# Attention over 16 head pairs on one core: five entries of the order of a pair are moved

## The reference, cut to what matters

```python
q   = (rmsnorm(xn @ q_a_w) @ q_b_w)             # 32 heads, 128 + 64 (rotated)
kv  = rmsnorm(ckv[:, :64]) @ kv_b_w             # latent of rank 64
scores = (q_nope . k_nope + rope(q_pe) . rope(k_pe)) * 192 ** -0.5
scores = where(topk_mask & causal, scores, -inf)
out = softmax(scores) @ v @ o_w
x + attention(xn) + experts(xn)
```

## Time and profile before

| | us |
|---|---|
| median of 3 runs | 1024.95 (1023.12 to 1027.54) |
| span of the profiled execution | 1021.7 |
| PE busy in it | 896.0 (88%) |
| DVE busy | 741.3 (73%) |
| ACT busy | 680.6 (67%) |
| POOL busy | 450.1 (44%) |
| attention, pairs 1 to 14, one round of two pairs | about 73 |

### The profile page before, as it was taken

One profiled execution on the slowest core, in us unless ns is written; L12 is line 12 of the kernel. 1 busy time (PEld: TensorE's weight loads), 2 busy tenths in 40 slices (PEclk: granted clock), 3 DMA queues, 4 the chain that ended last, 5 costly groups with the idle time before them and its releaser, 6 DMA issues.

```text
span 1021.7 us, 25695 instructions
## 1 busy us (share of the span) xinstructions
PE 896.0 (88%) x7912; PEld 548.5 (54%) x7912; DVE 741.3 (73%) x1593; ACT 680.6 (67%) x1512; POOL 450.1 (44%) x307
## 2 busy tenths in 40 slices
PE   5979999966764789998989989989989989989998
PEld 2434554434420266666666656656666656665443
DVE  5385699999999877876787777767767868783000
ACT  3656689977853488786777778768868868873000
POOL 2193239876548454363354436426335525600000
PEclk9999999997777899999999999999999999999999
DMA  7011111113344800000000000000000000220211
GB/s 223 22 36 57 52 48 57 41 36 99 100 147 157 305 23 22 2 23 23 22 3 23 22 3 22 22 3 22 22 8 17 22 23 2 90 98 22 62 41 41
DMA packets 47259, 52.67 MB, mean 52 GB/s; under 512 B 5440, under 2 KB 31424, under 8 KB 47168
## 3 DMA queue, kind: packets, MB, share of 16 engines
q1 hardware_dynamic: 47168, 51.31, 15.2%
HBM read 36.62 MB, written 6.29 MB: 42 GB/s over the span
## 4 chain that ended last, share of the span: by engine, by line
PE 50%; issue 18%; POOL 14%; DVE 11%; ACT 3%; DMA 1%; DVEq 1%; SPq 0%; ACTq 0%; POOLq 0%
PE psS L575 11%; PE psS L684 8%; PE psT L652 8%; PE psO L633 6%; POOL arena L1409 4%; PE psT L450 4%; DVE m L1103 3%; POOL arena L1411 3%; PE psS L474 3%; ACT arena L714 2%; PE psS L427 2%; POOL arena L1420 2%; POOL arena L1418 2%; DVE bias L1107 1%; PE psT L560 1%
## 5 line engine op out<-in xcount | busy, mean ns | idle before, releaser
L714 ACT ACTIVATE arena<-psT 128x512 f16<-128x512 f32 (+5 forms) x544 | 263.4, 519 | 145.5 <-PE psT L652 101.5
L968 DVE SCALAR_TENSOR_TENSOR arena<-psT,arena 128x512 f16<-128x512 f32 (+3 forms) x392 | 205.9, 553 | 89.1 <-ACT arena L714 89.1
L575 PE MATMUL psS<-keyT,arena 128*128 128x512 f16 (+3 forms) x1152 | 231.7, 329 | 13.8 <-POOL arena L1420 12.3
L1202 DVE CUSTOM_DVE_ANT_0 arena<-psS,bias 128x1024 f32<-128x1024 f32 (+7 forms) x256 | 192.6, 752 | 50.2 <-PE psS L575 48.0
L914 ACT ACTIVATE arena<-arena,small 128x1024 f32<-128x1024 f32 (+7 forms) x256 | 199.2, 778 | 18.4 <-DVE small L1202 15.8
L652 PE MATMUL psT<-ident,arena 128*128 128x128 f32 x1152 | 177.7, 281 | 26.8 <-issue 17.7
L633 PEld LDWEIGHTS psO<-val,arena 128*128 128x128 f16 x3456 | 132.6, 98 | 38.7 <-DVE arena L968 6.0
L575 PEld LDWEIGHTS psS<-keyT,arena 128*128 128x128 f16 x1152 | 104.2, 99 | 86.1 <-issue 34.1
L633 PE MATMUL psO<-val,arena 128*128 128x64 f16 x3456 | 143.9, 193 | 1.5 <-DVE arena L968 1.2
L652 PEld LDWEIGHTS psT<-ident,arena 128*128 128x128 f32 x1152 | 123.6, 141 | 32.0 <-issue 23.7
L1401 POOL TENSOR_TENSOR arena<-arena,cq 128x1024 f32<-128x1024 f32 x16 | 37.8, 2364 | 214.8 <-ACT arena L714 214.8
(11 more groups left out here) (146 smaller groups left out, 1111.4 us busy)
## 6 DMA issues: line engine op xcount, KB each, us to landing
arena<-in_wiq SPq DMA_DIRECT2D x32, 256.0 KB, 2.7
arena<-in_ow SPq DMA_DIRECT2D x16, 512.0 KB, 4.8
arena<-arena SPq DMA_DIRECT2D x32, 256.0 KB, 2.3
arena<-in_qbT SPq DMA_DIRECT2D x16, 256.0 KB, 2.5
wvo_parts<-arena SPq DMA_DIRECT2D x16, 256.0 KB, 4.6
arena<-in_qpe SPq DMA_DIRECT2D x16, 128.0 KB, 2.6
arena<-in_x SPq DMA_DIRECT2D x8, 256.0 KB, 2.7
out<-arena SPq DMA_DIRECT2D x8, 256.0 KB, 2.0
```

The source lines that it names most:

```text
L575: last = mm(psS[k % 2][:, c:c + w], Q[:, v, a, h, t * P:(t + 1) * P], keyT[:, b, h, c:c + w], start=(a, b) == (0, 0), stop=(a, b) == (1, 0))
L714: return nc.scalar.activation(dst, src, ACT.Copy, scale=scale)
L968: return v.scalar_tensor_tensor(out=dst, in0=src, scalar=scale, in1=hi, op0=ALU.mult, op1=ALU.subtract)
L1202: v.tensor_tensor_reduce(out=pr[:, k % 4, 0:kw], in0=psS[k % 2][:, 0:kw], in1=bias[:, TOFF[t]:TOFF[t + 1]], scale=-c_s, scalar=3e38, op0=A ...
```

## The change

The change edits the tables that set the order within a pair, and the order of POOL's parts. With it the query parts stand at steps 0, 1, 3 and 5, the result transposes at steps 7 and 9, the casts of the rotated high parts behind step 6, and POOL makes both latent low parts before the rotated ones.

```diff
         AHEAD = 3
-        ROPE_AT = 8
-        Q_AT, O_AT = {0: 0, 2: 1, 5: 2, 9: 3}, {4: 0, 8: 1}
+        ROPE_AT = 6
+        Q_AT, O_AT = {0: 0, 1: 1, 3: 2, 5: 3}, {7: 0, 9: 1}
...
                 q_low(p, v_, 2)
+                q_low(p, v_, 3)
                 rope_low(p, v_)
-                q_low(p, v_, 3)
```

## The result

| | before | changed |
|---|---|---|
| median, on the same chip | 1026.24 us (1023.12 to 1028.05, 4 runs) | 1039.86 us (1039.63 to 1040.99, 4 runs) |
| ratio | | 1.0147 (1.0123 to 1.0171) |
| span of the profiled execution | 1021.7 | 1039.1 |
| mean granted clock of PE | 0.965 | 0.952 |

The change made the kernel **slower by 1.5%, 13.6 us**; the forecast was slower by 10.6. The profiled spans differ by more, 17.4 us, since the profiled execution of before was the shortest of its four runs and that of the changed kernel the longest of its four.

What follows compares the result with a forecast made beforehand. PE, busy 88% of the span, was taken as the bound. Per pair, +0.26 us from the waits and DVE's queue plus 0.5 for held casts, over 14 pairs, gave 1024.95 + 10.6 = 1035.5 us; forecast range 1029 to 1040.

Steps and rivals of the forecast that it cites:

- The wait for POOL goes: At the next pair's first scores (step 13), PE no longer waits for POOL's last low part: gain 0.9 us per pair.
- Step 6 starts 1.23 later: Query parts moved up and waits for fresh banks at steps 3 and 5 start step 6 1.23 us later.
- Step 10 stands 9.01 behind step 6, by DVE's queue: Casts and first result precede step 8's chunks on DVE, so steps 6 to 10 take 9.01 us, winning only 0.07.
- The cast is held for 0.5: DVE's casts at step 6 meet POOL's latent part 3 and wait for its instruction: 0.5 us per pair.
- ACT's copy, a tie at no cost: ACT's copy of part 3 waits for POOL's part 2; both reach 807.1, so it costs nothing.
- The swap transfers cost nothing: SP's swap transfers move up 2.5 us with part 1; POOL waits 0.7 for them as before, no cost.
- the cast of 1.1 to 1.3 us: Sign in the profile: DVE's first cast takes 1.1 to 1.3 us, not 0.68, ending just behind a POOL instruction.
- the waits at steps 7 to 9 of over 1 us: Sign in the profile: PE waits for DVE's low parts at steps 8 and 9, over 1 us per pair in all.
- the distance of a round's pairs: Sign in the profile: the distance between rotations of a round's two pairs grows by 0.8 us.
- Rival A: No change within 0.5%: new bank waits and DVE's queue cost what the POOL wait gave, casts held little; chance 0.28.
- rival B: Faster: PE's queue decides, DVE has slack at steps 6 to 9, giving 1012 or 1007 us; chance 0.16.
- rival C: Much slower: casts held 1.15 us or by both POOL instructions, and ACT held by POOL, 1045 us; chance 0.06.

Runs made afterwards that it cites:

- experiment 3: The changed kernel with the result transposes back at steps 4 and 8: 1024.93 us, ratio 0.9987 to the kernel before.
- experiment 2: The changed kernel with POOL's old order, latent part 3 behind the rotated low part again: 1034.32 us, ratio 1.0083 to the kernel before.
- experiment 1: The changed kernel with the casts back at step 8: 1046.00 us, ratio 1.0184 to the kernel before.
- experiment 4: The changed kernel with results back at steps 4 and 8 and casts back at step 8: 1033.81 us, ratio 1.0080 to the kernel before.
- the best order: The kernel before with query part 1 at step 1, casts at step 4 behind the result's low part, POOL's rotated low part first: 1017.41 us, ratio 0.9912.
- experiment 6: The kernel before with POOL's order alone changed, both latent low parts ahead of the rotated one: 1061.85 us, ratio 1.0346.
- experiment 5: The kernel before with only the casts moved, from step 8 to step 6: 1041.55 us, ratio 1.0146.

## Why the prediction was right

It was right in direction, in size (+10.6 forecast, +13.6 measured, +10.2 in the pairs themselves) and in its main mechanism, DVE's queue. Part of the closeness is luck, as the sum below shows, and it left out the clock. Step by step:

1. *The wait for POOL goes, -0.9.* Right: the row is gone, and POOL is done 6.1 us ahead of step 13. It was worth more than its bracket: from step 10's transposes to step 13's scores it took 5.96 (821.02 - 815.06) with the wait and takes 4.91 (837.11 - 832.20) without, 1.05 for a bracket of 0.88.
2. *Step 6 starts 1.23 later.* 1.42 measured (15.96 into the pair, 14.54 before). A bank came free 2.14 and 2.05 us after its transposes began (814.86 - 812.72, 819.63 - 817.58), not 2.0, and the walk adds two such banks: that is the 0.19 by which the forecast was short. The wait at the query part of step 3 was 0.37 for 0.40. The one at step 5 is not in brackets, but part 3 starts 12.84 into the pair for the forecast 12.65.
3. *Step 10 stands 9.01 behind step 6, by DVE's queue.* With the casts' hold of item 4 that made 9.51; measured are 9.45. The chain was exact where it was a chain of DVE: the second result began 7.11 behind step 6 (829.86 - 822.75), the forecast's 6.89 and the hold's 0.22. Behind it the forecast had 2.12 and the trace has 2.34. Some 0.15 of these 0.22 is a wait that I missed: `head_out` (L1225) writes the tile that the transposes of the previous pair's result read, so it waits for the second of them, which now comes a step later. DVE idles 0.26 for it, and PE's values of step 8, which need the bank that `head_out` empties, begin at 831.50, 1.14 behind the scores where it is 0.98 to 1.01 in step 2 and in experiment 3. One figure beside the sum was misread: PE's own work there is not 7.4 but 7.8 (9.08 less the part's 1.29 and the two waits' 0.43, and 0.43 for the second result, which was forgotten). So the chain left PE 1.2 of waiting and not 1.6; measured are 1.27.
4. *The cast is held for 0.5.* The mechanism was right and the term mis-sized: **0.22**, with the hold measured twice, in the cast (898 and 680 ns) and in the pair (experiment 2). Two reasons. POOL began part 3 0.2 earlier against step 6 than I had it, so the overlap was 0.35 and not 0.55. And the cast ended 0.55 behind POOL's instruction (826.09 - 825.54), not its full 0.68, so that a hold is the overlap less 0.13. The cast of 0.76 in the earlier trace rows says the same (0.21 of overlap, 0.08 of hold): with it the forecast's own overlap would have cost 0.42. It was read as a bound, and the row of 1962 ns alone was used. The Trainium skill ("SBUF — State Buffer", section "Who interferes with whom") says that the one that comes later blocks until the other's instruction is done, and that issue order decides who blocks. The trace agrees with both, but for these 0.13.
5. *ACT's copy, a tie at no cost.* Right: ACT's three copies of part 3 take 1.69 in the pair at 806.79, as before.
6. *The swap transfers cost nothing.* Right: POOL waits 0.73 for them.

The sum of items 1 to 4 is +0.76 forecast and +0.73 measured, but the closeness is luck, owed to errors that cancel: 0.28 too much for the hold and 0.17 too little for the wait that went, against 0.41 too little for the later banks (0.19) and for what follows the second result (0.22). Of what the prediction named to look for, the cast of 1.1 to 1.3 us was not there (0.90); the waits at steps 7 to 9 of over 1 us were (1.27 with the one inside step 8), the distance of a round's pairs grew as forecast.

What it did not have at all is the clock at the loop's turn, 5.2 us in the profiles. The trace of before showed it: three turns of six at half clock. PE's stop of 3 us there ("issue" in the views: a wait with no cause that the profile shows) was taken as fixed, and what PE does behind it was not looked at.

It also put the blame less sharply than the runs do. It named the casts and the first result's low part together. Experiments 1, 3 and 4 part them: with the query parts and POOL's order changed, the casts at step 6 are a gain of 0.4 to 0.6 against step 8, and the results at 7 and 9 are a loss of 0.8 to 1.0. Rival A, no change, is what the change does without its third part, the results' move (experiment 3). No run that takes parts of the change came out faster as rival B had it (the query parts alone and the results alone were not run on the kernel before), and rival C's held ACT did not come about.

## What to carry to other kernels

When an engine's queue sets the pace in one stretch, ask of every moved piece whether it leaves that stretch or enters it. Work that feeds the next stage early is worth nothing if it stands ahead of the evacuation of a bank that PE waits for: here the best order puts DVE's movable work into its idle time, and behind whatever frees a bank. The total of a wait view does not price an order, as 0.2 of 0.8 us showed in it; distances between the same instruction in successive iterations do.

## What was not expected of the hardware

- PE's clock fell to its lower level behind waits that are short beside those at the turns: 2.2 us in one piece (experiment 6, ten pairs of 14), and 1.2 and 0.5 us with 0.7 of work between (experiment 5, five pairs of 14). A fall costs 1.3 to 1.6 us here (36.54 - 35.21 in experiment 5, 37.57 - 35.96 in experiment 6), more than most waits that the orders trade. Equal stops of 2.6 to 3.2 us at the turns were followed by a fall in three of six cases in one order and in all six in another.
- DVE's cast and POOL's tensor_tensor hold each other in both directions: a cast of 0.69 took 1.55, POOL's 1.15 took 1.50, and a POOL instruction of 2.13 takes 2.63 when the second cast runs beside it. A cast that started 0.1 before POOL's instruction ended was not held visibly. In all of them the hold is the overlap less 0.12 to 0.14: 0.08 for 0.21, 0.22 for 0.35, 0.35 for 0.48, 0.50 for 0.64 and 0.86 for 0.99.
